# Reordering the transform stages, the second projection and the odd-half copies in a fused Swin block and frequency-domain convolution (16 images)

## What is computed

```python
# block 1: a Swin block on 16 windows of 8 x 8, 8 heads of 16
t = layernorm(tok); q, k, v = split(t @ qkv_w.T + qkv_b)
out = softmax(q * scale @ k.T + rel_bias) @ v @ proj_w.T + proj_b
tok = tok + out
tok = tok + gelu(layernorm(tok) @ w1.T + b1) @ w2.T + b2
# block 2: a mixture of five routes of out0 = gelu(in_w * x)
h_out, v_out = depthwise 3x3 of dilated axis convolutions of out0
pyr   = depthwise 3x3 of four grouped 3x3 convolutions of out0, dilations 1, 6, 12, 20
x_sca = |ifft2(w1 * s * boosted fft2(w2 * s))| * alpha + s * beta,  s = scaled |out0|
out   = x + cw0*(1+edge)*h_out + cw1*(1+edge)*v_out + cw2*(1-0.3*edge)*pyr + cw3*point + cw4*x_sca
y     = out_w * relu(out) + out_b
```

## Time and profile before

| | us |
|---|---|
| median of 3 runs | 1525.22 |
| lowest, highest | 1523.16, 1525.64 |
| the profiled execution: its time | 1523.85 |
| the profiled execution: its span | 1521.6 |
| PE busy | 1365.2 |
| DVE busy | 1275.5 |
| ACT busy | 919.2 |
| POOL busy | 404.3 |

### The profile page before, as it was taken

How to read it: one execution, slowest core, us unless ns; L and a number is a source line. 1 busy time by engine, 2 the same in 40 slices (tenths; PEclk the granted TensorE clock), 3 DMA queues, 4 the chain that set the end, 5 groups by cost and what they waited for, 6 DMA issues and landing times.

```text
span 1521.6 us, 43439 instructions
## 1 busy us (share of the span) xinstructions
PE 1365.2 (90%) x17328; PEld 812.6 (53%) x17328; DVE 1275.5 (84%) x2376; ACT 919.2 (60%) x1717; POOL 404.3 (27%) x318
## 2 busy tenths in 40 slices
PE   5689899999999999999989899998999999899782
PEld 3346556464655556465564646555564555546360
DVE  4628888998989899898989989898898989898867
ACT  3474755667575566747556575755667575566541
POOL 4014050321505032150503215050330505023050
PEclk9989999999999999999999999999999999999986
DMA  4102012130201213030121302012130201212020
GB/s 164 25 16 77 4 44 63 17 91 16 71 26 46 58 17 91 15 84 11 42 65 17 90 16 64 29 41 67 17 90 16 64 29 34 60 17 77 3 76 14
DMA packets 32622, 70.93 MB, mean 47 GB/s; under 512 B 14116, under 2 KB 17188, under 8 KB 32068
## 3 DMA queue, kind: packets, MB, share of 16 engines
q1 hardware_dynamic: 32452, 68.27, 17.6%
HBM read 22.40 MB, written 9.08 MB: 21 GB/s over the span
## 4 chain that ended last, share of the span: by engine, by line
PE 46%; DVE 29%; DVEq 11%; ACT 8%; issue 5%; DMA 1%; SPq 0%; ACTq 0%
PE bank L628 8%; PE bank L638 7%; DVE row_max L1079 4%; PE bank L500 4%; PE bank L761 3%; PE bank L564 3%; DVE score L1081 3%; PE bank L519 3%; DVEq L1078 3%; PE bank L718 3%; DVE hv L1209 3%; DVE score L1076 2%; PE bank L588 2%; ACT fft L1533 2%; PE bank L793 2%
## 5 line engine op out<-in xcount | busy, mean ns | idle before, releaser
L761 PE MATMUL bank<-act,mats_sb 128*32 128x512 f32 (+15 forms) x2592 | 215.1, 421 | 0.0
L1209 DVE SCALAR_TENSOR_TENSOR hv<-ver,mix,hv 128x1024 f32<-128x1024 f32 x144 | 185.0, 1285 | 11.1 <-issue 0.4
L1917 POOL TENSOR_TENSOR resT<-xT,proj_shift 128x1024 f32<-128x1024 f32 x16 | 37.8, 2360 | 522.0 <-DVE x1T L1101 516.7
L1209 DVE SCALAR_TENSOR_TENSOR hv<-hor,mix,hv 128x1024 f32<-128x1024 f32 x128 | 164.4, 1285 | 11.0
L1937 POOL TENSOR_SCALAR hor<-act,cols_sb 128x1024 f32<-128x1024 f32 x16 | 26.7, 1666 | 486.4 <-ACT act L1620 427.2
L761 PEld LDWEIGHTS bank<-act,mats_sb 128*32 128x32 f32 x2592 | 121.7, 110 | 50.1 <-issue 29.0
L564 PE MATMUL bank<-k_heads,qC 128*64 128x512 f32 x512 | 139.6, 623 | 5.6 <-DMA k_heads<-kC 3.9
L1947 POOL TENSOR_SCALAR axis_part<-act,cols_sb 128x320 f32<-128x320 f32 (+1 forms) x128 | 136.7, 1068 | 21.6 <-issue 21.6
L1574 ACT ACTIVATE score<-score 128x512 f32<-128x512 f32 x128 | 79.4, 631 | 94.9 <-DVE score L1081 94.5
L1579 ACT ACTIVATE probT<-bank 128x512 f32<-128x512 f32 x128 | 77.3, 604 | 96.9 <-PE bank L577 96.8
L1076 DVE TENSOR_TENSOR score<-bank,rel_bias 128x512 f32<-128x512 f32 x128 | 87.2, 682 | 51.9 <-PE bank L564 51.2
(11 more groups left out here) (187 smaller groups left out, 2747.6 us busy)
## 6 DMA issues: line engine op xcount, KB each, us to landing
pyr_stack<-pyr SPq DMA_DIRECT2D x96, 144.2 KB
x_in<-x_dram SPq DMA_DIRECT2D x16, 512.0 KB, 4.9
k_heads<-kC SPq DMA_DIRECT2D x128, 64.0 KB, 2.4
edge<-edge_dram SPq DMA_DIRECT2D x16, 512.0 KB, 4.1
out_dram<-y_out SPq DMA_DIRECT2D x16, 512.0 KB, 3.6
k_heads<-rel_dram SPq DMA_DIRECT2D x2, 1024.0 KB, 12.9
mats_sb<-mats_dram SPq DMA_DIRECT2D x1, 1978.5 KB, 7.4
pyr_stack<-pyr SPq DMA_DIRECT2D x16, 123.2 KB
```

The costliest lines, as they stand in the source:

```text
L761: last = pe.matmul(to, w_pyr[:, d, t], act[:, y0 + dy:y1 + dy, x0 + dx:x1 + dx], start=(t == 4), stop=(t == PYR_ORDER[8]), skip_group_chec ...
L1209: last = dve.scalar_tensor_tensor(hv[:], src, mix[:, a, k:k + 1], hv[:], ALU.mult, ALU.add)
```

## The change

PE and ACT have one place in a slot instead of two (`conv_slot`), behind `value_turn` and `value_copy`, so that the next pair's scores lie between two transform stages. `x2_conv` stays in slot 1, ahead of the scores; `turn_even`, `turn_odd` and `last_even` go from the slots to the tail. `project(i, 0)` goes to the tail and `project(i, 1)` ahead of `pyramid_conv(n, 0)`. The four copies of the odd half go from DVE to ACT. On DVE both halves of `norm1_stats` stand in slot 1, `bias_max` stands ahead of the transform work, two taps more lie ahead of the MLP, and `square_sum` goes ahead of `norm2(i, 1)`. On ACT `first_tap` goes from slot 1 to slot 4, `edge_cuts` to a place between `deviation2(i, 1)` and `normalise2(i, 1)`, and a one-element square root (`first_gelu`) is added at the end of slot 5.

```diff
-        SLOT_TAPS = (1, 1, 1, 1, 1, 1, 1, 2, 3, 3, 5)
+        SLOT_TAPS = (1,1,1,1,1,1,1,2,4,5,7)
# PE
+            def conv_slot(n, j):
+                if j == 2:
                     dft_rows(n)
                 elif j == 3:
+                    turn_spectrum(n)
+                elif j == 4:
                     r_even(n)
                 elif j == 5:
+                    dft_columns(n)
+                    r_odd(n)
+                elif j == 6:
                     inverse_even(n)
                 elif j == 7:
+                    inverse_odd(n)
...
                 for j in range(PAIRS):
-                    conv_early(n, j)
+                    if j == 1:
+                        pyramid(n, 4)
+                        x2_conv(n)
                     if j + 2 < PAIRS:
                         scores(i, j + 2)
                     prob_transposes(i, j, f)
...
                     if j >= 2:
                         value_turn(i, j - 2)
-                    conv_late(n, j)
-                    if j == 7:
-                        project(i, 0)
+                    conv_slot(n, j)
                     if j == 1:
                         pe.wait_ge(given_sb, 2 * n + 2)
                     values(i, j)
+                turn_even(n)
                 value_turn(i, 6)
+                project(i, 0)
+                turn_odd(n)
+                last_even(n)
+                value_turn(i, 7)
                 last_odd(n)
-                value_turn(i, 7)
+                project(i, 1)
                 pyramid_conv(n, 0)
-                project(i, 1)
                 pyramid_conv(n, 1)
# DVE
                 for j in range(1, PAIRS):
-                    if j in (4, 5):
-                        conv_slot(n, j)
                     scale_values(i, j - 1)
-                    if j in (1, 2) and f is not None:
-                        norm1_stats(f, j - 1)
-                    if j >= 6:
-                        conv_slot(n, j)
                     if j == 1:
+                        if f is not None:
+                            norm1_stats(f, 0)
+                            norm1_stats(f, 1)
                         mix_input(n)
-                    elif j == 3:
-                        r_even_bias(n)
                     if j + 2 < PAIRS:
                         bias_max(i, j + 2)
                     if j == 1:
                         sum_edge(n)
-                    elif j == 2:
+                    elif j == 3:
                         mix_magnitudes(n)
+                    elif j == 4:
+                        r_even_bias(n)
+                    elif j == 5:
+                        boosted(n)
+                        even_product(n)
+                    elif j == 6:
+                        odd_product(n)
                     taps(n, range(SLOT_TAPS[j], SLOT_TAPS[j + 1]))
                 scale_values(i, 7)
                 residual_stats(i, 0)
+                taps(n, range(SLOT_TAPS[PAIRS], SLOT_TAPS[PAIRS + 1]))
                 norm2(i, 0)
-                taps(n, range(SLOT_TAPS[PAIRS], SLOT_TAPS[PAIRS + 1]))
                 residual_stats(i, 1)
+                square_sum(n)
                 norm2(i, 1)
-                square_sum(n)
# ACT
+            def inverse_odd_copy(n):
+                act_.wait_ge(go_sb, 2 * n + 2)
+                for k in range(2):
+                    act_.wait_ge(ao_ps, 2 * n + k + 1)
+                    copy(other_tile(fb, k), tile_rows(bank[4 + k])).then_inc(ao_sb, 1)
+            def turn_odd_copy(n):
+                for k in range(2):
+                    act_.wait_ge(to_ps, 2 * n + k + 1)
+                    copy(half(fd, k), bank[4 + k][:]).then_inc(to_sb, 1)
...
                 for j in range(PAIRS):
+                    if j == 1:
+                        given_copy(n)
+                        pyr_copy(n, 1)
+                        x2_copy(n)
+                    elif j == 2:
+                        edge_tanh(n)
                     prob_copy(i, j)
...
                     if j >= 2:
                         value_copy(i, j - 2)
+                    conv_slot(n, j)
                     if j + 2 < PAIRS:
                         exponent(i, j + 2)
+                    if j == 5:
+                        act_.activation(first_gelu[:], ones[:, 0:1], ACT.Sqrt)
+                turn_even_copy(n)
                 value_copy(i, 6)
+                turn_odd_copy(n)
+                value_copy(i, 7)
+                square_even(n)
+                deviation2(i, 0)
                 square_odd(n)
-                value_copy(i, 7)
-                deviation2(i, 0)
                 normalise2(i, 0)
                 deviation2(i, 1)
+                edge_cuts(n)
                 normalise2(i, 1)
```

More of the change, by code:

```diff
@@ L931, in both @@
                     prob_transposes(i, j, f)
+                    if j == 0:
+                        if late is not None:
+                            pe.wait_ge(z_copied, n + 1)
+                            pe.wait_ge(xs_sb, 2 * n + 1)
+                            out_conv(late)
+                        pyramid(n, 3)
                     if j >= 2:
                         value_turn(i, j - 2)
[L934 to L937, removed]
-                    conv_late(n, j)
-                    if j == 7:
-                        project(i, 0)
+                    conv_slot(n, j)
                     if j == 1:
@@ L1242, in odd_product @@
                     dve.tensor_tensor(fd[:, h], bank[4 + k][:], fb[:, h], ALU.mult).then_inc(go_sb, 1)
[L1244 to L1254, removed]
             def mix_input(n):
@@ L1317, in conv_slot @@
                     odd_product(n)
[L1318 to L1321, removed]
             def swin_rest(i, f):
@@ L1761, in out_copy, with conv_slot @@
                                     bias=col("out_b")).then_inc(out_sb, 1)
-            def conv_early(n, j):
-                if j == 0:
-                    pyr_copy(n, 0)
-                elif j == 1:
+            def conv_slot(n, j):
+                if j == 2:
+                    row_spectrum_copy(n)
+                elif j == 3:
+                    spectrum_turn_copy(n)
+                elif j == 4:
                     first_tap(n)
-                elif j == 2:
-                    edge_tanh(n)
-                    row_spectrum_copy(n)
-                elif j == 5:
+                elif j == 6:
                     inverse_even_copy(n)
-                elif j == 6:
-                    turn_even_copy(n)
                 elif j == 7:
-                    square_even(n)
-            def conv_late(n, j):
-                if j == 1:
-                    given_copy(n)
-                    pyr_copy(n, 1)
-                    x2_copy(n)
-                elif j == 2:
-                    spectrum_turn_copy(n)
-                elif j == 6:
-                    edge_cuts(n)
+                    inverse_odd_copy(n)
             def swin_rest(i, f):
@@ L1856, in conv_only @@
                 route_exponent(n)
-                for j in range(PAIRS):
-                    conv_early(n, j)
-                    if j == 0:
-                        out_copy(n - 1)
-                    conv_late(n, j)
+                out_copy(n - 1)
+                pyr_copy(n, 0)
+                given_copy(n)
+                pyr_copy(n, 1)
+                x2_copy(n)
+                edge_tanh(n)
+                for j in range(PAIRS):
+                    conv_slot(n, j)
+                edge_cuts(n)
+                turn_even_copy(n)
+                turn_odd_copy(n)
+                square_even(n)
                 square_odd(n)
```

29 lines of the change are left out of this document (5 added, 24 removed).

## The result

The changed kernel takes 1466.47 us (median of four runs, 1465.81 to 1467.95), the kernel before 1524.84 (four runs, 1523.16 to 1525.64): a ratio of 0.962, 95% interval 0.9603 to 0.9637. The forecast was 1490 with a range down to 1474, so the direction was right and the gain, 58 us instead of 35.5, lay outside the range. The profiled execution took 1465.89 us, its span 1463.7.

What follows compares the result with a forecast made beforehand. PE and DVE were taken to bound the kernel in turns. Savings of 23.8 us over 14 turns, 7.3 where conv_only begins and 4.4 at its end made 35.5, so 1490 us; own range 1479 to 1502, wider range 1474 to 1517.

Steps and rivals of the forecast that it cites:

- What bounds the kernel: Whole turn: PE and DVE take turns; DVE is full up to `even_product`, then project, `residual_stats`, `norm2`, `normalise2` count.
- Slots: Slots 1 to 6: shorter `mix_input` (1.5), new waits such as 1.2 ahead of `scores(i, 4)`, even product ready at 776.05.
- The tail: Behind the slots: `project(i, 1)` done at 787.3, not 791.1; `normalise2` at 794.15, not 796.10; PE's wait 1.7 becomes 1.0.
- The POOL collision: In the tail: `square_sum` is held by POOL's `residual_in`, 2.35 long, ending at 790.75, so it ends at 791.95.
- The sum for a turn: Each turn of `both`: 1.95 saved by `normalise2`'s end, 1.55 by waits; 1.7 taken, bounds 1.0 and 2.4, 23.8 over 14.
- with the clock full in both: PE's own work in a turn: at full clock in both kernels, a moved stage costs PE what it cost before.
- The ends: Where `conv_only` begins, 7.3 us saved (bounds 5.3 and 8); at its end, 4.4 (bounds 3.6 and 4.8).
- The load in slot 5: The 1.28 us table load ahead of the first deviation moves from the tail to slot 5, where ACT is idle.
- A: Rival, tail: `square_sum` isn't held by POOL, PE waits no more, 2.7 a turn saved, 1476 us; chance 0.15.
- B: Rival, loop: wait ahead of `scores(i, 4)` grows by 1.7, only 11.7 us saved outside the loop, 1514 us; chance 0.17.
- C: Rival, slower: squares among square roots need four table loads, 5.1 us; 2.3 lost a turn, 1550 us; chance 0.08.
- the slots' start gains nothing: Slots 1 and 2: two old PE waits, 2.3 us, become new ones of the same 2.3.

Runs made afterwards that it cites:

- before: The kernel without the change: 1524.84 us, median of four runs.
- after: The changed kernel, with the whole change against the kernel before: 1466.47 us, ratio 0.962.
- b_three: Kernel before with its own slot order, plus odd-half copies on ACT, project(i, 1) ahead, value_copy(i, 7) ahead of square_odd, early square root in slot 5: 1524.44 us.
- b_copies: Kernel before with only the four copies of the odd half moved from DVE to ACT: 1516.37 us against 1525.56.
- u_copies: Changed kernel with the four copies of the odd half put back on DVE: 1557.19 us.
- b_project: Kernel before with only project(i, 1) moved ahead of both pyramid_conv on PE: 1512.84 us against 1523.18.
- p_slot3: Changed kernel with one more whole-image addition on DVE in slot 3, its result unused: 1487.24 us.
- b_two: Kernel before with its own slot order, odd-half copies on ACT, project(i, 1) ahead, value_copy(i, 7) ahead of square_odd, no early square root: 1507.64 us against 1518.73.
- v_race_sq: Changed kernel with two more POOL waits so DVE's mirrors go first, and square_sum behind norm2(i, 1): 1452.97 us, 0.9537 of the kernel before.
- v_race: Changed kernel with two more POOL waits so that DVE's even and odd mirrors go first: 1459.64 us, 0.9589 of the kernel before.
- v_square: Changed kernel with square_sum moved back behind norm2(i, 1) on DVE: 1463.43 us.
- u_load: Changed kernel without the one-element square root in slot 5, so the table load stands in the tail again: 1496.56 us.
- d_cuts: Changed kernel with edge_cuts run three times in a row ahead of normalise2(i, 1) on ACT: 1508.10 us.
- u_project: Changed kernel with project(i, 1) put back between the two pyramid_conv: 1528.83 us.

## Why the prediction was wrong, point by point

**What bounds the kernel: right.** DVE up to `even_product`, PE and the chain of `norm2` behind it. The lengthened list of slot 3 shows the first, the three runs on the wait for `normalise2` the second.

**Slots: right in kind, each term a little too long.** From the turn's start (731.5 in the turn of the prediction), in a typical turn of full clock: `mix_input` took 1.35 where 1.5 was taken; `scores(i, 4)` waited 0.7, not 1.2. `values(i, 1)` waited the 0.8 of the forecast, `inverse_even` 0.6 (0.2), `values(i, 2)` 0.4 (0.3) and `values(i, 7)` not at all (0.35). The even product was ready at 44.2, not 44.55.

**The tail: right in kind, too long again.** `project(i, 1)` ended at 55.4 (forecast 55.8), `norm2` at 60.1 (60.95; in before 62.9), the wait for `normalise2` was 0.6 (1.0). The POOL collision came, but earlier: `residual_in` ended at 58.7 and not 59.25, and `square_sum` 1.1 behind it.

**The step that failed: "The sum for a turn", 1.7 with bounds 1.0 and 2.4.** In typical turns it is 2.8 (88.9 to 86.1), above the bound, and all of it is there at the end of `norm2`: in n = 8 of both kernels it ended at 62.96 and at 60.12, and the way from there to the next turn is 25.95 in both. By its own path the prediction had 1.95; the 0.9 that it missed are 0.4 at the end of `project(i, 1)` and the rest in the chain behind it. By the waits it had 1.55: those that went were 5.5, the new ones are 3.0 where 3.85 were forecast, so 2.5 are saved. The remaining 0.35 are PE's own busy time (83.2 to 83.0), held to be the same, and gaps of less than 0.15. Guesses that nearly all leaned the same way were added as if each were the middle, and their other side was never summed. Then the falls of the clock, in 4 of 14 turns at about 1.4, or 0.4 in the mean, were priced at nothing: "with the clock full in both" was read from one turn. The turns in which the mirrors go first take a little of that back, so the mean is 3.07, and 14 x 1.37 = 19 of the missing 22.5 us are this step.

**The ends: right mechanism, low size.** 15.0 us instead of 11.7. For the last `both` and `conv_only`'s beginning 7.3 was taken, with a bound of 8, and they gave 9.6: the last `both` itself 2.7, where the sum had 1.3 for its tail, the gap its whole 4.55 with no wait left, and the slow part 2.07 (0.3 more lie in the small products there). The end of `conv_only` saved 4.8, for which 4.4 was taken, and 0.6 lie ahead of the first turn.

**The load in slot 5, "where ACT is idle": right for this order of the slots, and worth 30 us.** The prediction had ACT not last in the tail and gave the load no price of its own; at full clock it is 1.2 us of a turn, and the falls that it keeps away come on top. In the old order the same load costs 17 us.

**The rivals.** A named a turn's saving of 2.7, near the measured one, but by another cause, so the nearness is luck: `square_sum` was held by POOL all the same. B and C did not come: no wait in the slots is above 0.8, and the squares ran behind the root's load without a load of their own: three loads a turn in both kernels.

**That parts add up** was taken throughout. For the copies and the projection on before it holds in typical turns (0.15 and 0.5, together 0.6). With the load it is false: on the kernel with both it costs 17 us, on after it brings 30. And undone on after, each by itself costs 91, 62 and 30 us, 183 for a change that brings 58. What lets them pay is probably the part that the prediction priced at nothing ("the slots' start gains nothing"): one stage in a slot with scores in between, so that neither ACT nor DVE has a full stretch ahead of a PE stage. That is argued from the timelines of b_three and not shown: the new order alone, without the other moves, was not tried, nor was the load alone on before.

## What to carry to other kernels

Read the granted clock of every turn, not of one, and look for PE's longest wait in it: shortening that wait can give back more than its length. Price a schedule as a whole: the same table load cost 17 us on one order of the slots and brought 30 on another, so test a move by undoing it on the new kernel as well as by doing it alone on the old. When several unknown terms are taken on the safe side, sum the other side too, for that sum is the bound of the range.

## What the runs showed of the hardware

**The clock falls behind short waits.** Every fall in the turns n = 0 to 13 of these kernels began within 2 us of the end of a PE wait of 1.7 us or more, and but for one (a second fall in n = 0 of b_copies) it was the turn's longest, wherever that wait was put; a fall cost PE about 1.3 us, and in u_copies (3.0 us) up to 2.7. Turns of n = 0 to 13 with a granted clock below 0.99, by the longest wait in a typical turn. Turn n = 0 has a longer one of its own in some kernels: the single fall of b_project, and one each of b_copies, p_slot3 and b_three, stood there, behind 2.0 to 2.4 us, while b_two had none in it behind 1.8. Past these turns a wait of 1.5 was enough once (n = 14 of p_slot3).

| kernel | longest wait, us | turns with a fall |
|---|---|---|
| after | 0.8 | 0 |
| v_race_sq | 0.8 | 0 |
| v_race, v_square | 0.8, 0.8 | 0, 0 |
| b_two | 1.2 | 0 |
| b_project | 1.2 | 1 |
| before | 1.7 | 4 |
| b_copies | 1.7 | 3 |
| p_slot3 | 1.7 | 5 |
| u_load | 1.7 | 7 |
| d_cuts | 2.0 | 12 |
| b_three | 2.6 | 6 |
| u_copies | 3.0 | 14 |
| u_project | 3.1 | 13 |

Length isn't all: with the same wait of 1.7 us, 10 of the 14 turns of before had no fall, and 2.6 us in slot 6 gave fewer falls than 2.0 us in the tail. What else decides stays open.

**Two operations that begin some 0.03 us apart go either way, and 1 us of a turn hangs on it.** DVE's even mirror and POOL's sum begin that close together (in n = 7 of before at 742.63 and 742.59). In n = 1 to 13 of both kernels the sum's record begins first, by 0.03 to 0.06 us, and yet the mirror went first in 3 turns of before and 4 of after; by which of them is held, here or at the odd mirror, the turn is 88.1 or 88.9 in before. What decides it the traces don't show; that the order is what costs, v_race shows. The one that is held lasts until the other is through, even where it has 15 elements (1.51 us instead of 0.18). The Trainium skill, page "SBUF — State Buffer", section "SBUF: two separate sides", calls the port pair that both share a lock held for a whole instruction and not a split of bandwidth. By that rule, the traces agree: `square_sum` took 2.30, of which 1.22 passed before POOL's operation ended, and the last 1.08 are nearly its own 1.21.
